# Statistics of two row tiles moved from VectorE to ScalarE, silu moved behind the first four statistics, and new orders for all engines

## The chip, the core and the metric

The kernel runs on one core of one Trainium2 chip. The metric is the device time of one execution in microseconds (us); of the kernel before there are three runs: 1036.51, 1036.54 and 1036.72 us, median 1036.54 us. Times inside the kernel are those of one profiled execution, counted from the start of its span.

## What is computed

The reference is one AdaLN block in fp32 over x of shape (4, 1024, 1024): a modulation, attention with one head of 256, and a linear layer with a low-rank addition. What matters here is the front:

```python
mod = (_silu(L0_c) @ L0_wmod).reshape(L0_c.shape[0], 6, 1, -1)
sa, ca, ga, sb, cb, gb = (mod[:, 0], mod[:, 1], mod[:, 2], mod[:, 3], mod[:, 4], mod[:, 5])
h = _layernorm(x, axis=-1) * (1 + ca) + sa          # mean and variance of each row
x = x + ga * _L0_attn_ref(h, Wqkv, bqkv, Wo, bo)    # q, k, v = h @ Wqkv + bqkv; softmax; Wo
h = _layernorm(x, axis=-1) * (1 + cb) + sb
x = x + gb * _L0_ffn_ref(h, ...)
```

## The kernel before

Each batch b (0 to 3) has eight row tiles t of 128 rows by 1024, in two chunks j of four tiles. Each fp32 product is made of three fp32r products, of high and low parts: ScalarE writes the high part (rounded), VectorE the low part (what is left), and TensorE multiplies high by high, low by high and high by low (lines 1420 to 1422). Every engine follows a list of steps written out by hand (PE_ORDER, DVE_ORDER, ACT_ORDER, SP_ORDER, POOL_ORDER; TensorE's entries also name one of four PSUM pairs, A to D, and the step that must have been emptied out of it). An engine takes its steps strictly in this order, and each waits on semaphores, so a step that waits holds back all that stand behind it.

The steps that matter for the front of the kernel, batch 0:

- SP_ORDER loads 512 KB at a time: LN (b, t) a row tile of x (line 799, places xs, probs and xr), Lwm (s, k) a piece of the modulation weights (line 783 for the scale, named s = 0 in the order, line 785 for the others), LT a piece of x with columns on the partitions (line 819), LWq a piece of Wqkv (line 790), LW of Wo (line 858). The first 57 SP steps end with LN (1, 4).
- VectorE: SI makes silu of c (lines 1141 to 1143), which TensorE needs for M0 (0); ST (b, t) makes mean and variance of a row tile (two bn_stats of 512 columns, line 1221, a bn_aggr, line 1224; semaphore stat_made); Z (b, j, k) subtracts the mean and multiplies by 1/std (lines 1239, 1243); MM0 (c) brings a quarter of the scale into place (line 1147, semaphore ca_made); WQL the low part of the weights (lines 1207, 1210); HL the low part of h (line 1249); BQ the biases of q, k, v.
- ScalarE: WQH the high part of weights (line 1014), MC0 copies the scale out of PSUM (line 993), HH the high part of h (line 1026), BMC and BPC copy the spread means and 1/std of chunk 1 (line 1001), KR copies k out of PSUM (line 1053), EX the exponentials of the softmax (line 1090).
- GpSimd: RS (b, j) makes 1/std of a chunk (lines 929, 931).
- TensorE: BCM (j) and BCP (j) spread mean and 1/std of chunk j over the partitions (line 1487; BCM (j) waits for the four statistics of the chunk, and chunk 0 includes tiles 0 to 3, chunk 1 tiles 4 to 7); M0 (c) and MT0 (c) make and turn a quarter of the scale (lines 1443, 1454); K0 (c) and V0 (c) are quarters of k and v of chunk 0 (lines 1567 and 1420 to 1422); M (s, r) and MT (s) make and turn the other modulation rows (lines 1465, 1473; r = 0 needs pieces 0 and 1, r = 1 pieces 2 and 3); Q, K, V (b, j, ...) are q, k, v; SAM and SAT the share of the shift in the biases; S, PT, PV and O the attention; PP and W the low-rank weights; T and F the second norm's turn and the last product.

The first V0 waits until the second quarter of the scale has left its PSUM pair (ca_made at least 2). The front runs, on TensorE: BCM0, M0 0, BCP0, MT0 0, M0 1, K0 0, MT0 1, M0 2, V0 0, MT0 2, K0 1, V0 1, M0 3, V0 2, MT0 3, K0 2, BCP1, BCM1, V0 3, M 1 0, M 1 1, Q 0 0 0 and so on.

## Time and profile before

| what | value |
|---|---|
| runs | 1036.51, 1036.54, 1036.72 us; median 1036.54 |
| the profiled execution | 1036.71 us, of which its span is 1034.9 |
| TensorE (PE) matmul busy | 1007.2 us, 97% of the span |
| VectorE (DVE) busy | 660.2 us, 64% |
| ScalarE (ACT) busy | 312.3 us, 30% |
| GpSimd (POOL) busy | 235.7 us, 23% |
| granted TensorE clock | 0.997 of full speed |

The page gives busy time for each engine; PE is the matmuls, PEld the weight loads beside them, SPq the DMA issues of the sync engine. In a timeline row the first number is the start, the second the duration in us, then engine, line, operation, output and inputs, and in brackets how long the engine was idle before it and what ended that.

### The profile page before, as it was taken

To read this page: it belongs to the slowest core of one execution; us is meant where nothing else is said; L and a number is where in the kernel's file an instruction comes from. 1 tells how busy PE (TensorE), PEld (TensorE's weight loads), DVE (VectorE), ACT (ScalarE), POOL (GpSimd) and SP (SyncE) were. 2 spreads that over 40 slices of the span, in tenths; PEclk is the share of its full clock that TensorE was granted. 3 is DMA by queue.
4 is the path that set the end of the run, shared out by engine and by line. 5 is a ranking of instruction groups with operands and counts; after the bars stand their busy time and mean duration, and the time that the engine had idled before them with its cause. 6 is when DMAs were issued, how large, how long until landed. Compare 5 with 4: busy or idle time off the path is not lost.

```text
span 1034.9 us, 13028 instructions
## 1 busy us (share of the span) xinstructions
PE 1007.2 (97%) x5213; PEld 830.1 (80%) x5213; DVE 660.2 (64%) x830; ACT 312.3 (30%) x468; POOL 235.7 (23%) x181
## 2 busy tenths in 40 slices
...
GB/s 364 391 325 304 250 241 135 281 235 188 59 1 161 125 198 128 1 112 133 142 151 142 49 153 233 220 146 224 185 222 84 247 178 183 128 231 157 114 78 65
DMA packets 54428, 180.23 MB, mean 174 GB/s; under 512 B 5872, under 2 KB 6432, under 8 KB 54368
## 3 DMA queue, kind: packets, MB, share of 16 engines
...
q8 instruction: 42, 0.69, 0.3%
q14 instruction: 18, 0.15, 0.1%
...
## 4 chain that ended last, share of the span: by engine, by line
PE 94%; SPq 2%; DMA 2%; DVE 1%; issue 0%; ACT 0%; DVEq 0%; ACTq 0%
PE pairA L1420 8%; PE pairA L1421 8%; PE pairA L1422 8%; PE pairD L1420 7%; PE pairD L1421 7%; PE pairD L1422 7%; PE pairC L1420 7%; PE pairC L1421 7%; PE pairC L1422 7%; PE pairB L1420 6%; PE pairB L1422 6%; PE pairB L1421 6%; DMA w_raw<-in_wqkv 2%; SPq L819 1%; PE pairB L1617 1%; PE pairB L1552 1%
## 5 line engine op out<-in xcount | busy, mean ns | idle before, releaser
L956 POOL TENSOR_TENSOR res<-res,row_bc 128x1024 f32<-128x1024 f32 x32 | 84.2, 2640 | 85.4 <-DMA res<-x_dram 76.7
L943 POOL TENSOR_TENSOR xr<-xr,row_bc 128x1024 f32<-128x1024 f32 x32 | 81.2, 2544 | 92.8 <-DMA xr<-in_x 92.3
L1420 PE MATMUL pairD<-w_hi,h_hi 128*128 128x256 f32 (+1 forms) x256 | 87.0, 340 | 0.0
L1421 PE MATMUL pairD<-w_lo,h_hi 128*128 128x256 f32 (+1 forms) x256 | 86.6, 338 | 0.0
L1422 PE MATMUL pairD<-w_hi,h_lo 128*128 128x256 f32 (+1 forms) x256 | 86.3, 337 | 0.0
L948 POOL DMA_DIRECT2D x_dram<-xr x32 | 18.1, 567 | 258.6 <-DVE xr L1326 258.6
L1420 PE MATMUL pairC<-w_hi,h_hi 128*128 128x512 f32 (+1 forms) x192 | 72.3, 377 | 3.2 <-DVE h_lo L1249 2.7
L1421 PE MATMUL pairC<-w_lo,h_hi 128*128 128x512 f32 (+1 forms) x192 | 71.9, 375 | 0.0
L1422 PE MATMUL pairC<-w_hi,h_lo 128*128 128x512 f32 (+1 forms) x192 | 71.7, 373 | 0.0
L1117 ACT ACTIVATE w_hi<-w_sum 128x1024 fp32r<-128x1024 f32 x32 | 33.9, 1060 | 119.6 <-DVE w_sum L1370 119.3
L1421 PE MATMUL pairA<-w_lo,h_hi 128*128 128x256 f32 (+1 forms) x192 | 65.0, 338 | 0.0
L1420 PE MATMUL pairA<-w_hi,h_hi 128*128 128x256 f32 (+1 forms) x192 | 64.8, 338 | 0.0
L1422 PE MATMUL pairA<-w_hi,h_lo 128*128 128x256 f32 (+1 forms) x192 | 64.8, 337 | 0.0
L1026 ACT ACTIVATE h_hi<-z_cols,modT 128x512 fp32r<-128x512 f32 x64 | 42.7, 715 | 42.3 <-DVE z_cols L1243 37.5
L1411 DVE TENSOR_TENSOR res<-res,gated 128x1024 f32<-128x1024 f32 x31 | 53.0, 1711 | 0.8 <-POOL res L956 0.3
L1420 PEld LDWEIGHTS pairD<-w_hi,h_hi 128*128 128x128 f32 x256 | 48.3, 189 | 5.8
L1421 PEld LDWEIGHTS pairD<-w_lo,h_hi 128*128 128x128 f32 x256 | 48.4, 189 | 5.5
L1422 PEld LDWEIGHTS pairD<-w_hi,h_lo 128*128 128x128 f32 x256 | 48.3, 189 | 5.5
L965 POOL DMA_DIRECT2D out_y<-res x31 | 23.4, 756 | 124.5 <-DVE res L1411 124.5
L1420 PE MATMUL pairB<-w_hi,h_hi 128*128 128x512 f32 x128 | 50.3, 393 | 0.0
L1422 PE MATMUL pairB<-w_hi,h_lo 128*128 128x512 f32 x128 | 50.1, 392 | 0.0
L1421 PE MATMUL pairB<-w_lo,h_hi 128*128 128x512 f32 x128 | 50.1, 392 | 0.0
...
## 6 DMA issues: line engine op xcount, KB each, us to landing
...
```

Source lines behind the costliest of these rows:

```text
L819: sp.dma_start(z_cols[j][:, c2, :], x_cols[b, j, :, c2, :]).then_inc(ld_cols[j][k], 16)
L943: nc.gpsimd.tensor_tensor(xt, xt, row_bc[:, :], ALU.add).then_inc(residual_made, 1)
L948: pool.dma_start(x1_dram[row:row + P, :], xr[:, t % 2, :]).then_inc(st_x1[t % 2], 16)
L956: nc.gpsimd.tensor_tensor(rt, rt, row, ALU.add).then_inc(residual2_made, 1)
L965: pool.dma_start(dst.rearrange("(t p) n -> p t n", p=P), res[:, slot, :].rearrange("p (t n) -> p t n", t=2)).then_inc(st_y[slot], 16)
L1026: nc.scalar.activation(h_hi[j][:, ct, :], z_cols[j][:, ct, :], ACT.Copy, scale=modT[:, PLACE[CA], b, ct:ct + 1]).then_inc(h0_hi_made, 1)
L1117: nc.scalar.activation(w2_hi[h][:, 2 * cp:2 * cp + 2, :], w_sum[:, n % 2, :].rearrange("p (c n) -> p c n", c=2), ACT.Copy).then_inc(w2_hi_ ...
L1411: nc.vector.tensor_tensor(res[:, slot, :], res[:, slot, :], gated[:, :], ALU.add).then_inc(y_made, 1)
L1420: nc.tensor.matmul(out, left[0], right[0], start=first, stop=False, skip_group_check=True)
L1421: nc.tensor.matmul(out, left[0], right[1], start=False, stop=False, skip_group_check=True)
L1422: return nc.tensor.matmul(out, left[1], right[0], start=False, stop=last, skip_group_check=True)
L1552: last = nc.tensor.transpose(ps[:, (2 * cc + k) * P:(2 * cc + k + 1) * P], xs[:, k, ct * P:(ct + 1) * P], ident)
```

## The change

VectorE gives up the statistics of tiles 5 and 7 of batch 0. ScalarE makes them in five instructions each: a copy of the tile onto itself that also sums it, mean and negated mean from the sum, a square of the tile minus its mean that also sums, and the variance. It uses two new semaphores and three columns of `total` as scratch. Since stat_made then counts 30 statistics and not 32, its waiters take their number from stat_no, and those that need tiles 5 or 7 also wait for act_stat_made. SI stands behind the first four ST on VectorE. All five orders are new: 414 steps of TensorE, 268 of SP and 152 of GpSimd are the same steps in another order. SP's first 57 steps stay in place.

```diff
+        ACT_STATS = (5, 7)
+        def stat_no(b, t):
+            return QT * b + t - sum(QT * b + t > k for k in ACT_STATS)
...
                 elif what == "LN":
-                        sp.wait_ge(stat_made, 6 if (b, t) == (1, 0) else QT * b + t)
+                        if (b, t) == (1, 0):
+                            sp.wait_ge(act_stat_made, 1)
+                        else:
+                            sp.wait_ge(stat_made, stat_no(b, t))
...
                 if what == "RS":
-                    pool.wait_ge(stat_made, QT * b + 4 * j + 4)
+                    pool.wait_ge(stat_made, stat_no(b, 4 * j + 4))
+                    if b + j > 0:
+                        pool.wait_ge(act_stat_made, 2)
...
+                elif what == "ST":
+                    t = i[1]
+                    place, turn = stat_place(0, t)
+                    no = ACT_STATS.index(t)
+                    rows = rows_at[place]
+                    act.wait_ge(ld_rows[place], 16 * turn)
+                    wait(act, act_stat_made, no)
+                    nc.scalar.activation(rows, rows, ACT.Copy, accum_out=sums[:, 0:1]).then_inc(act_stat_step, 1)
+                    act.wait_ge(act_stat_step, 4 * no + 1)
+                    nc.scalar.activation(stat[:, 1, 0, t % 4:t % 4 + 1], sums[:, 0:1], ACT.Copy, scale=1.0 / H).then_inc(act_stat_step, 1)
+                    nc.scalar.activation(sums[:, 1:2], sums[:, 0:1], ACT.Copy, scale=-1.0 / H).then_inc(act_stat_step, 1)
+                    act.wait_ge(act_stat_step, 4 * no + 3)
+                    nc.scalar.activation(rows, rows, ACT.Square, bias=sums[:, 1:2], accum_out=sums[:, 2:3]).then_inc(act_stat_step, 1)
+                    act.wait_ge(act_stat_step, 4 * no + 4)
+                    nc.scalar.activation(stat[:, 1, 1, t % 4:t % 4 + 1], sums[:, 2:3], ACT.Copy, scale=1.0 / H).then_inc(act_stat_made, 1)
...
                     if what == "BCM":
-                        pe.wait_ge(stat_made, 4 * j + 4)
+                        pe.wait_ge(stat_made, stat_no(0, 4 * j + 4))
+                        if j == 1:
+                            pe.wait_ge(act_stat_made, 2)
```

The front of three orders, as it becomes. TensorE:

```python
    ("BCM", (0,), "A", None), ("M0", (0,), "B", None), ("BCP", (0,), "A", None), ("MT0", (0,), "B", None),
    ("M0", (1,), "C", None), ("K0", (0,), "D", None), ("M0", (2,), "B", ("M0", 0)), ("MT0", (1,), "C", None),
    ("MT0", (2,), "B", None), ("V0", (0,), "C", ("M0", 1)), ("M0", (3,), "B", ("M0", 2)), ("K0", (1,), "D", None),
    ("MT0", (3,), "B", None), ("V0", (1,), "C", None), ("K0", (2,), "D", None), ("V0", (2,), "C", None),
    ("BCM", (1,), "A", ("BCM", 0)), ("K0", (3,), "D", None), ("BCP", (1,), "A", None),
    ("M", (1, 0), "B", ("M0", 3)), ("M", (1, 1), "B", None), ("Q", (0, 0, 0), "D", ("K", 0, 0)),
    ("M", (1, 2), "B", None), ("V0", (3,), "C", None), ("M", (1, 3), "B", None), ("Q", (0, 0, 1), "D", None),
```

VectorE (before, MM0 (1) stood ahead of WQL (1, 1), HL (0, 0, 3) behind WQL (0, 0)):

```python
    ("ST", (0, 0), None), ("ST", (0, 1), None), ("ST", (0, 2), None), ("ST", (0, 3), None), ("SI", (), None),
    ("Z", (0, 0, 0), "A"), ("MM0", (0,), "B"), ("WQL", (1, 0), None), ("HL", (0, 0, 0), None),
    ("WQL", (2, 0), None), ("Z", (0, 0, 1), "A"), ("WQL", (1, 1), None), ("MM0", (1,), "C"), ("MM0", (2,), "B"),
    ("HL", (0, 0, 1), None), ("Z", (0, 0, 2), "A"), ("WQL", (2, 1), None), ("ST", (0, 4), None),
    ("HL", (0, 0, 2), None), ("ST", (0, 6), None), ("Z", (0, 0, 3), "A"), ("MM0", (3,), "B"),
    ("HL", (0, 0, 3), None), ("WQL", (0, 0), None), ("WQL", (0, 1), None), ("Z", (0, 1, 0), None),
    ("Z", (0, 1, 1), None), ("ST", (1, 0), None), ("Z", (0, 1, 2), None), ("Z", (0, 1, 3), None),
```

Later on VectorE: ... VL (0, 1, 0), ST (1, 3), BQ, QL (0, 0, 0), ... ScalarE (before, WQH (0, 0) stood ahead of HH (0, 0, 3)):

```python
    ("WQH", (1, 0), None), ("MC0", (0,), "B"), ("HH", (0, 0, 0), None), ("WQH", (2, 0), None), ("MC0", (1,), "C"),
    ("WQH", (1, 1), None), ("MC0", (2,), "B"), ("HH", (0, 0, 1), None), ("WQH", (2, 1), None), ("MC0", (3,), "B"),
    ("HH", (0, 0, 2), None), ("ST", (0, 5), None), ("ST", (0, 7), None), ("HH", (0, 0, 3), None),
    ("WQH", (0, 0), None), ("WQH", (0, 1), None), ("BMC", (1,), "A"), ("KR", (0, 0, 0), "D"),
```

The last dozen steps of TensorE and the last dozen of VectorE are those of before, with other PSUM pairs, but for WL2 (3, 7), which changes place with a neighbour.

## Rows read from the trace of the kernel before

**Rows 1.** The page, busy time by engine.
```profile
PE 1007.2 (97%) x5213; PEld 830.1 (80%) x5213; DVE 660.2 (64%) x830; ACT 312.3 (30%) x468; POOL 235.7 (23%) x181
```

**Rows 2.** Waits of PE, whole span: us in total, times, longest.
```profile
PE pairA L1487 <- DVE stat L1224: 11.8, 1, 11.8
PE pairC L1420 <- DVE h_lo L1249: 2.7, 2, 1.6
PE pairD L1567 <- ACT h_hi L1026: 1.9, 1, 1.9
PE pairA L1643 <- DVE q_lo L1318: 0.5, 1, 0.5
...
PE pairC L1652 <- DVE w_sum L1370: 0.4, 1, 0.4
PE pairC L1420 <- DVE w_sum L1370: 0.4, 1, 0.4
```

**Rows 3.** Timeline of PE, start to 52 us: start, duration, instruction, idle before.
```profile
11.85 2.04 PE L1487 MATMUL pairA<-consts,stat 128*128 128x128 f32 x8 [11.85 <-DVE stat L1224]
...
25.26 0.39 PE L1420 MATMUL pairC<-w_hi,h_hi 128*128 128x256 f32 x1 [0.50 <-DVE modT L1147]
...
28.23 0.50 PE L1454 MATMUL pairB<-consts,row_bc 128*128 128x4 f32 x4
28.60 1.17 PE L1567 MATMUL pairD<-h_hi,w_hi 128*128 128x512 f32 x4
...
31.47 0.28 PE L1420 MATMUL pairC<-w_hi,h_hi 128*128 128x256 f32 x1
...
49.43 1.92 PE L1465 MATMUL pairB<-wm,pads 128*32 128x512 f32 x16
51.28 0.50 PE L1420 MATMUL pairA<-h_hi,w_hi 128*128 128x512 f32 x1
```

**Rows 4.** Timeline of VectorE, to 80 us.
```profile
5.98 1.28 DVE L1221 BATCH_NORM_STATS2 bn<-xs 128x6 f32<-128x512 f32 x2
...
25.04 0.16 DVE L1147 TENSOR_SCALAR modT<-pairC 128x8 f32<-128x8 f32 x1
25.72 1.23 DVE L1210 TENSOR_TENSOR w_lo<-w_raw,w_hi 128x1024 fp32r<-128x1024 f32 x1 [0.52 <-ACT w_hi L1014]
...
33.63 1.28 DVE L1221 BATCH_NORM_STATS2 bn<-xs 128x6 f32<-128x512 f32 x2
...
79.93 0.69 DVE L1221 BATCH_NORM_STATS2 bn<-xs 128x6 f32<-128x512 f32 x1 [9.38 <-DMA xs<-in_x]
```

**Rows 5.** Timeline of ScalarE: high part of weight piece (1, 1).
```profile
24.63 1.06 ACT L1014 ACTIVATE w_hi<-w_raw 128x1024 fp32r<-128x1024 f32 x1 [2.65 <-DMA w_raw<-in_wqkv]
```

**Rows 6.** Single lines: issues, first and last start, then time from issue to landing.
```profile
L799 SPq DMA_DIRECT2D xs<-in_x x1: 389/389/389, 0.7 to 0.7; - x1
...
DMA to landing us min/median/max: 4.0/4.4/4.8
```

**Rows 7.** The same for the fifth and sixth scale pieces, window 8.2 to 8.7.
```profile
L783 SPq DMA_DIRECT2D wm<-in_w_scale x2: 434/454/475, 7.8 to 8.3; - x2
DMA to landing us min/median/max: 14.2/14.6/15.0
```

**Rows 8.** The same for the last two of Lwm (1, 0) to (1, 3).
```profile
L785 SPq DMA_DIRECT2D wm<-in_wmod x2: 1076/2482/3887, 30.1 to 34.0; - x2
DMA to landing us min/median/max: 15.0/16.3/17.6
```

**Rows 9.** Timeline of SP's issues: row tile LN (1, 3).
```profile
71.10 0.45 SPq L799 DMA_DIRECT2D xs<-in_x  x1
```

**Rows 10.** Groups by line and shape, ScalarE: busy us, mean ns.
```profile
L1090 ACT ACTIVATE probs<-pairA,neg_max 128x1024 f32<-128x1024 f32 x9 | 10.0, 1114 | 9.8 <-DVE neg_max L1305 9.8
...
L1090 ACT ACTIVATION_READ_ACCUMULATOR probs<-pairA,neg_max 128x1 f32 x9 | 1.8, 197 | 0.0
...
L1123 ACT ACT_TABLE_LOAD x1 | 1.3, 1283 | 1.2 <-PEq L1678 1.2
```

More of the change, by code:

```diff
@@ L394 @@
     ("LT", 1, 0, 3), ("Lwm", 2, 4), ("Lwm", 2, 5), ("LN", 1, 3), ("Lwm", 2, 6), ("Lwm", 2, 7), ("LN", 1, 4),
-    ("Lwm", 3, 0), ("Lwm", 3, 1), ("SW", 1, 0), ("Lwm", 3, 2), ("Lwm", 3, 3), ("LN", 1, 5), ("LBC", 1, 0),
-    ("Lwm", 3, 4), ("Lwm", 3, 5), ("Lwm", 3, 6), ("Lwm", 3, 7), ("LN", 1, 6), ("Lwm", 4, 0), ("Lwm", 4, 1),
-    ("LN", 1, 7), ("RS_", 0), ("Lwm", 4, 2), ("Lwm", 4, 3), ("LN", 2, 0), ("Lwm", 4, 4), ("RS_", 1), ("Lwm", 4, 5),
-    ("SW", 1, 1), ("Lwm", 4, 6), ("Lwm", 4, 7), ("LN", 2, 1), ("LBC", 1, 1), ("Lwm", 5, 0), ("Lwm", 5, 1),
-    ("Lwm", 5, 2), ("Lwm", 5, 3), ("LN", 2, 2), ("Lwm", 5, 4), ("Lwm", 5, 5), ("LN", 2, 3), ("Lwm", 5, 6),
[14 rows of a table removed]
-    ("LW2", 1, 0), ("LRES", 0, 1, 0, 0), ("LW2", 1, 1), ("LRES", 0, 1, 0, 1), ("LRES", 0, 0, 1, 0),
[10 rows of a table removed]
+    ("SW", 1, 0), ("LN", 1, 5), ("LBC", 1, 0), ("LN", 1, 6), ("Lwm", 3, 0), ("Lwm", 3, 1), ("Lwm", 3, 2),
+    ("Lwm", 3, 3), ("LN", 1, 7), ("Lwm", 3, 4), ("Lwm", 3, 5), ("Lwm", 3, 6), ("Lwm", 3, 7), ("LN", 2, 0),
+    ("SW", 1, 1), ("RS_", 0), ("Lwm", 4, 0), ("Lwm", 4, 1), ("Lwm", 4, 2), ("LBC", 1, 1), ("Lwm", 4, 3),
+    ("LN", 2, 1), ("Lwm", 4, 4), ("Lwm", 4, 5), ("LN", 2, 2), ("Lwm", 4, 6), ("Lwm", 4, 7), ("Lwm", 5, 0),
+    ("Lwm", 5, 1), ("LN", 2, 3), ("Lwm", 5, 2), ("Lwm", 5, 3), ("Lwm", 5, 4), ("Lwm", 5, 5), ("LN", 2, 4),
[19 rows of a table added]
+    ("LRES", 1, 1, 1, 0), ("LX", 9), ("LW2", 2, 4), ("LRES", 1, 1, 1, 1), ("LRES", 2, 0, 0, 0),
[5 rows of a table added]
     ("LRES", 3, 0, 1, 0), ("LRES", 3, 0, 1, 1), ("LRES", 3, 1, 1, 0), ("LRES", 3, 1, 1, 1),
@@ L499, in build_block @@
         r_total = sb("r_total", [P, QT])
+        sums = total[:, 0:3]
         xs = sb("xs", [P, 2, H])
@@ L625, in build_block @@
         stat_made = sem("stat_made")
+        act_stat_made = sem("act_stat_made")
+        act_stat_step = sem("act_stat_step")
         stat_spread = sem("stat_spread")
@@ L823, in step @@
                     if n == 0:
-                        sp.wait_ge(stat_made, QT * B)
+                        sp.wait_ge(stat_made, stat_no(B, 0))
                         sp.wait_ge(z_made, 2 * 4 * B)
```

9 lines of the change are left out of this document (5 added, 4 removed), and 676 rows, old and new, of tables (ACT_ORDER, DVE_ORDER, PE_ORDER, POOL_ORDER).

## The prediction

> **What bounds the kernel now.** Read the page first: TensorE is busy for 1007.2 of 1034.9 us [rows 1], so an edit can only bring back the other 27.7 us, or add to them. The waits of TensorE say where they are [rows 2]: 11.8 us before its first matmul, then 1.9 + 0.5 + 2.7 = 5.1 us, each of them before its Q (0, 0, 0) at 51.28 [rows 3] (the 0.5 stands in the bracket of the row at 25.26), then 0.5 + 0.4 + 0.4 = 1.3 us around 590 to 627, where batch 3 ends and the F steps begin. The rest, 9.5 us, is nearly all the tail behind the last matmul; the last steps don't change, so it stays. From 51.28 to the first of the three late waits TensorE never waits: there the change can only lose. So I look at the time at which TensorE begins Q (0, 0, 0): before it stands, before and after, the same work but for two exchanges named below, and all that follows moves with it.
>
> The second reading is who feeds TensorE until then, and that is the DMA queue. Pieces of 512 KB are issued early and land long after, one every 1.3 us: the fifth and sixth scale pieces, issued at 7.8 and 8.3, land at 22.0 and 23.3 [rows 7]. The last piece that M (1, 1) needs is issued at 34.0 and lands at 49.0 [rows 8], and M (1, 1) stands just ahead of Q (0, 0, 0) in both orders. The issues up to there are the same and none is delayed, so with its last quarter (two matmul groups of 1.85 us for both M steps, 49.43 to 51.28 [rows 3], so 0.5 us for the last piece) Q can't begin before 49.5. **The most that the front can give is 51.28 - 49.5 = 1.8 us.**
>
> **Part 1: SI behind the first four statistics.** The first tile lands at 0.7 + 4.0 = 4.7 [rows 6], but the first statistics start at 5.98 [rows 4], behind SI, which waits for the exponential. From there to BCM (0) are 11.85 - 5.98 = 5.9 us. Started at 4.75, BCM (0) starts at 10.6: 1.25 us sooner. SI (0.7 us) then ends at 11.2, and M0 (0), its only user, comes behind BCM (0) (2.04 us [rows 3]), at 12.6: hidden by 1.4 us.
>
> **Part 2: the order of TensorE up to the first V0.** K0 (0) can go earlier, since MM0 (0) no longer stands behind a WQL: the 1.9 us wait goes. But M0 (2) now comes before MT0 (1), and waits for its pieces until 23.3. Then V0 (0) waits until MM0 (1) has emptied the pair, and on VectorE MM0 (1) now stands behind WQL (1, 1), whose weights land at 24.6: ScalarE 24.63, VectorE 25.72, 1.14 us until the next can start [rows 4, 5], so MM0 (1) at 26.86 and, with its 0.16 us and the hand-over (25.04 to 25.26 before [rows 3, 4]), **V0 (0) at 27.1 and not at 25.26: a new wait, 1.8 us later**. Queued behind WQL (1, 1) and MM0 (1) on VectorE are MM0 (2) and HL (0, 0, 1), for which M0 (3) and K0 (1) wait; they have V0 (0)'s 3.0 us of cover. MT0 (2) (0.4) is done inside the wait. So the gain of part 1 is lost here and comes back only with the later waits.
>
> **Part 3: from V0 (0) to Q.** Before, 51.28 - 25.26 = 26.0 us, of them 2.7 us waits for h_lo [rows 2], so 23.3 us work. After: less MT0 (2), 28.23 to 28.60, 0.37; V0 (3) is behind Q and K0 (3) ahead of it: less 2.97 (25.26 to 28.23), plus 2.87 (28.60 to 31.47) [rows 3]. That makes 22.85 us. Do the 2.7 us go? The first wait was for HL (0, 0, 2), behind two statistics; now one stands before it, and TensorE comes 0.8 us later. The second was for HL (0, 0, 3), behind WQL (0, 0) and so behind the landing of its weights; that is undone. What is late next is ScalarE: HH (0, 0, 3), BCM (1) and RS (0, 1) now wait for its statistics. No row shows a square with a sum. The nearest is the exponential over 1024 columns, 1.11 us, and its accumulator read, 0.2 [rows 10]; two of those and three small ones of some 0.2 to 0.3 give 3.5 us for a tile. At the low end (no reads) it is 3.1, at the high end a table load of 1.28 [rows 10] lies before each square and one behind it: 6.1. Tile 5 is there at 33.6 [rows 4] and tile 7 sooner than ScalarE is free, so both end at 40.6 (39.8 to 45.8 at the ends). TensorE comes to BCM (1) at about 43.2, counted back from Q at 50 through two M, BCP, K0 (3) and BCM: **covered by 2.6 us** at the middle value, short by 2.6 at the high end. LN (1, 0), which waits for ScalarE's tile 5 (37), stands in a DMA queue that is full until 49 anyway. The 2.8 us that VectorE is spared cost and save nothing by themselves: they are cover. So Q begins at 27.1 + 22.85 = 49.95, 0.45 after the DMA's bound: **1.3 us sooner**.
>
> **Part 4: the rest of the orders.** BPC (1) now comes behind K0 (3) and two KR, so Z (0, 1, 0) starts some 1.5 us later than before; HL (0, 1, 3) is wanted by V (0, 1, 0) behind SAM, and I find about 1 us of cover there. The three late waits: PP (0, 1) stood right behind PV (3, 0, 1) and is moved off, so 0.5 us goes; W (0, 3) and then O (3, 4) still follow the first WS closely, with two W's and the low part of O crowding before it, so I leave the 0.8 us and add 0.3. Net 0.2, not counted. SP's steps behind the 57th move by up to eight places, mostly row tiles ahead of modulation weights; POOL's by four at most (RS (3, 1) later); their users are tens of us away.
>
> **Sum.** The profiled execution is 1036.71 us, 1.8 more than its span. Span 1034.9 - 1.3 = 1033.6, execution 1035.4; the median of the runs is 0.17 lower, so **1035.2 us**, a gain of 0.13%. About 0.2% (2.07 us) is what a measurement of this kernel can tell from no change; I forecast less than that.
>
> **Rivals.**
> - *The late waits go as well, or TensorE packs better* (the new orders everywhere are for that): 1.3 to 1.8 in the front and all 1.3 later is 2.6 to 3.1 us, 1033.4 to 1033.9. For: PP's wait is undone. Against: the DMA's bound, and WS is still close.
> - *The gain is eaten by small new waits* past 51 us, where none were and 400 TensorE steps are in a new order: a few of 0.4 (the size seen for W) give 1036 to 1037. For: so many edits at so little idle.
> - *The row tile ahead of the biases*, ending slower. On VectorE ST (1, 3) now stands before BQ, and through QH and QL everything of q and k in batch 0 hangs on it; K (0, 1, 0) can't enter its pair before. Before, tile LN (1, 3) was issued at 71.1 [rows 9] and ST (1, 3) waited 9.4 us, until 79.93 [rows 4], at no cost. Now I step ST (1, 3) to 78.7, and TensorE to K (0, 1, 0) at 85.8, with 1.4 us of cover. A landing later than 80.1 costs TensorE each us; it must be past 81.4 to make the kernel slower and past 83.5 for over 0.2%. With an issue 2 to 4 us later than before (behind ST (1, 2)) it lands at 82 to 84; if the like happens in the next batch, 1037.5 to 1039.5. For: the 8.8 us from issue to landing. Against: the transfers before it are freed sooner.
> - *The square isn't in the loaded table.* The trace has one table load, of 1.28 us, for exponentials and copies together [rows 10]. If each square brings a load before and one after, ScalarE ends at 45.8, BCM (1) costs 2.6 us, and the kernel ends at 1037.8 (slower by 1.3). The Trainium skill, "ScalarE: Activation LUTs", section on table sets, speaks against this part of the change: functions come in sets with one expensive function each and cheap ones as filler, and a switch costs about 2.66 us with the drain; it doesn't say that square is among the fillers. By that figure, an estimate, four switches make 10.6 us, ScalarE ends at 51.2 and the kernel at 1043. No run shown here has a switch. The chance of this rival, 0.07, rests on rows: copies and exponentials of the whole kernel share one load.
>
> **How the numbers follow.** Forecast (1034.5 to 1036.1) 0.50; late waits too 0.15; gain eaten 0.15; row tile 0.13, of it 0.10 beyond 0.2%; table 0.07, of it 0.04 beyond. Faster by over 0.2%: 0.15. Slower: 0.10 + 0.04 = 0.14. Same: 0.71. The range reaches into the first rival and to the middle of the third: 1033.6 to 1038.2, which leaves out about 0.05 below and 0.10 above.
>
> **What would show it.** In the changed kernel's timeline: BCM (0) at 10.6; V0 (0) at 27.1 with a wait for modT of some 0.6 behind MT0 (2); no wait from there to Q (0, 0, 0) at 49.5 to 50; ScalarE's two tiles in 7 us with no second ACT_TABLE_LOAD; waits of TensorE for W at about 0.8 to 1.1. I am wrong if wmod's fourth piece lands at another time than 49.0, if there is a wait of TensorE between 51 and 590 of over 0.5 us, or if TensorE's busy time changes by more than 0.5 us by the order alone.

## The result, and the profile after

The changed kernel is slower: 1038.55 us median against 1036.71 us of the kernel before measured beside it, ratio 1.0015 (95% interval 1.0008 to 1.0022). The forecast was 1035.2, range 1033.6 to 1038.2, so the time lies outside the range and on its slow side. By the bound of 0.2% named there the change counts as within it; the sign and the size that I forecast are wrong. The profiled execution took 1038.47 us with a span of 1036.7; the forecast for it was 1035.4. So 3.07 us have to be found. One of the eleven timed runs of e10_fill7 took 3992 us and is left out everywhere below, which makes its median 1035.44 and not 1035.81.

The page of the kernel after, busy time by engine [rows 1]:

```profile
PE 1009.9 (97%) x5213; PEld 832.7 (80%) x5213; DVE 650.9 (63%) x822; ACT 318.5 (31%) x482; POOL 230.4 (22%) x181
```

TensorE has the same 5213 instructions and is busy for 2.7 us more. Nothing was added to it, so something took longer; what it was, this number doesn't say (e11_no_wait2 has 2.6 us more without the cause found here). The waits of TensorE over the whole span (total, times, longest), which answer to [rows 2]:

```profile
PE pairA L1520 <- DVE stat L1255: 10.8, 1, 10.8
PE pairB L1485 <- ACT row_bc L1007: 1.6, 1, 1.6
PE pairC L1474 <- DMA wm<-in_w_scale: 1.3, 2, 0.6
PE pairB L1474 <- DMA wm<-in_w_scale: 1.2, 2, 0.6
PE pairB L1650 <- ACT probs L1121: 1.1, 1, 1.1
PE pairB L1451 <- DVE w_sum L1401: 0.4, 1, 0.4
PE pairD L1451 <- DVE w_sum L1401: 0.4, 1, 0.4
PE pairA L1685 <- DVE w_sum L1401: 0.4, 1, 0.4
PE pairC L1451 <- DVE xr L1357: 0.3, 1, 0.3
```

The waits for h_lo are gone, as is the one for q_lo. New are the waits for the scale pieces (2.5 us), the one of 1.55 us before MT0 (2), and, late in the kernel, one of 1.1 us for the probabilities. The timeline of TensorE, from its first matmul to Q (0, 0, 0), which answers to [rows 3]:

```profile
10.79 0.98 PE L1520 MATMUL pairA<-consts,stat 128*128 128x128 f32 x3 [10.79 <-DVE stat L1255]
...
26.30 0.98 PE L1485 MATMUL pairB<-consts,row_bc 128*128 128x4 f32 x4 [1.55 <-ACT row_bc L1007]
27.27 0.58 PE L1451 MATMUL pairC<-w_hi,h_hi 128*128 128x256 f32 x1
27.65 0.42 PE L1452 MATMUL pairC<-w_lo,h_hi 128*128 128x256 f32 x1
27.87 0.41 PE L1453 MATMUL pairC<-w_hi,h_lo 128*128 128x256 f32 x1
...
32.31 1.06 PE L1474 MATMUL pairB<-wm,pads 128*32 128x256 f32 x15
...
51.74 0.50 PE L1451 MATMUL pairD<-h_hi,w_hi 128*128 128x512 f32 x1
```

The start is as forecast: BCM (0) at 10.79 (10.6), V0 (0) at 27.27 (27.1). Then it goes wrong inside V0 (0): its matmuls of 256 columns follow each other at 0.21 us instead of 0.12, MT0 (2) ahead of it takes 0.98 us where it took 0.50 [rows 3], and V0 (0) lasts from 27.27 to 32.31, 5.04 us, where it lasted 25.26 to 28.23, 2.97 us. The same stretch by windows; the last columns are the granted clock, the DMA share and GB/s. Of the kernel before:

```profile
24.00:26.00 2.00, 1.50 (x22) 0.93 (x15) 1.48 (x3) 1.37 (x2) 0.00 (x0) 1.00 1.03 420
26.00:28.00 2.00, 2.00 (x19) 2.00 (x18) 2.00 (x3) 1.18 (x3) 0.00 (x0) 1.00 1.02 408
```

and of the kernel after:

```profile
22.00:24.00 2.00, 1.07 (x16) 0.34 (x16) 1.97 (x3) 0.00 (x0) 0.00 (x0) 1.00 1.01 414
24.00:26.00 2.00, 0.74 (x8) 0.52 (x4) 0.51 (x2) 1.18 (x2) 0.00 (x0) 0.74 1.04 418
26.00:28.00 2.00, 1.70 (x7) 1.66 (x8) 1.38 (x3) 0.84 (x3) 0.00 (x0) 0.50 1.03 410
28.00:30.00 2.00, 2.00 (x12) 2.00 (x10) 1.93 (x3) 0.70 (x3) 0.00 (x0) 0.50 1.03 410
30.00:32.00 2.00, 2.00 (x12) 2.00 (x12) 1.97 (x3) 1.00 (x1) 0.00 (x0) 0.56 1.03 406
```

TensorE's granted clock goes from 2.4 to 1.2 GHz (0.50) in the window 24 to 26 and comes back in the window 30 to 32. With 0.74 and 0.56 as means of the two levels, that is 1.04 us at half in the first and 1.76 us in the last: low from 25.0 to 31.8. Just before it, TensorE worked 1.07 of 2 us and then sat in the new wait, which begins at 24.75: MT0 (2) needs ScalarE's copy MC0 (2) (25.79), and that stands behind WQH (1, 1), whose weights ScalarE could take only at 24.82. In the profile of the kernel before the clock stays at 1.00 there. The Trainium skill, "TensorE: Matmul & The Clock Gate", section "What's actually happening", says that a gate halves the array's clock by how busy the engine has been of late; by that rule a wait has a second price behind it, and this trace agrees. It doesn't come behind every wait, as e3 shows below.

The other loss is late. ScalarE around 567 us, start, duration, instruction, idle before:

```profile
564.38 1.03 ACT L1126 ACTIVATE h_hi<-pairB 128x1024 fp32r<-128x1024 f32 x1 [1.49 <-PE pairB L1650]
567.64 1.06 ACT L1135 ACTIVATE a_stack<-a_raw 128x1024 fp32r<-128x1024 f32 x1 [2.23 <-DMA b_raw<-in_lora_b]
568.60 1.04 ACT L1136 ACTIVATE b_stack<-b_raw 128x1024 fp32r<-128x1024 f32 x1
569.55 1.09 ACT L1121 ACTIVATE probs<-pairC,neg_max 128x1024 f32<-128x1024 f32 x1
```

The step TLA (both copies of the LoRA rows) now stands ahead of EX (3, 2). It waits for a transfer and then copies, 4.2 us in all, the exponentials stand behind it, and TensorE comes to the transposes of the probabilities 1.08 us too early. In the order of before the same wait of TLA is longer (3.7 us) but stands behind EX (3, 3), and TensorE has other work.

**The account of the profiled execution.** Q (0, 0, 0) at 51.74 instead of the 49.95 forecast: 1.79. Waits of TensorE behind 52 us: 1.08 + 0.30 + 0.39 + 0.40 + 0.44 = 2.61 instead of 1.33: 1.28. Together 3.07, the whole of the difference.

### The profile page after: what moved, and what is told of

Same layout as the page of the kernel before. It is cut to its first block, busy times and chain, and to the rows that moved or that the text cites. A ratio compares the mean times of both kernels' runs of the same rounds, so it can differ in the third digit from the quotient of the medians.

```text
span 1036.7 us, 13036 instructions
## 1 busy us (share of the span) xinstructions
PE 1009.9 (97%) x5213; PEld 832.7 (80%) x5213; DVE 650.9 (63%) x822; ACT 318.5 (31%) x482; POOL 230.4 (22%) x181
## 4 chain that ended last, share of the span: by engine, by line
PE 91%; DMA 4%; DVE 2%; issue 1%; SPq 1%; ACT 0%; POOL 0%; DVEq 0%; ACTq 0%; POOLq 0%
PE pairC L1451 8%; PE pairC L1452 8%; PE pairC L1453 8%; PE pairA L1452 7%; PE pairA L1451 7%; PE pairA L1453 7%; PE pairB L1451 6%; PE pairB L1452 6%; PE pairB L1453 6%; PE pairD L1451 6%; PE pairD L1452 6%; PE pairD L1453 6%; DMA w_raw<-in_wqkv 2%; DMA xs<-in_x 1%; PE pairD L1585 1%
## 5 line engine op out<-in xcount | busy, mean ns | idle before, releaser
L1451 PE MATMUL pairA<-w_hi,h_hi 128*128 128x512 f32 (+1 forms) x256 | 90.4, 353 | 0.0
L1452 PE MATMUL pairA<-w_lo,h_hi 128*128 128x512 f32 (+1 forms) x256 | 89.9, 351 | 0.0
L1453 PE MATMUL pairA<-w_hi,h_lo 128*128 128x512 f32 (+1 forms) x256 | 89.8, 351 | 0.0
L1451 PE MATMUL pairB<-w_hi,h_hi 128*128 128x512 f32 (+1 forms) x208 | 71.6, 344 | 0.4 <-DVE w_sum L1401 0.4
L1452 PE MATMUL pairB<-w_lo,h_hi 128*128 128x512 f32 (+1 forms) x208 | 71.3, 343 | 0.0
L1453 PE MATMUL pairB<-w_hi,h_lo 128*128 128x512 f32 (+1 forms) x208 | 71.1, 342 | 0.0
L1451 PEld LDWEIGHTS pairA<-w_hi,h_hi 128*128 128x128 f32 x256 | 48.3, 189 | 6.7
L1453 PEld LDWEIGHTS pairA<-w_hi,h_lo 128*128 128x128 f32 x256 | 48.3, 189 | 6.7
L1452 PEld LDWEIGHTS pairA<-w_lo,h_hi 128*128 128x128 f32 x256 | 48.4, 189 | 6.5
L1280 DVE SCALAR_TENSOR_TENSOR h_lo<-z_cols,modT,h_hi 128x512 fp32r<-128x512 f32 x64 | 44.3, 745 | 2.5 <-ACT h_hi L1056 2.5
```

What stands on the lines that cost most here:

```text
L1280: nc.vector.scalar_tensor_tensor(h_lo[j][:, ct, :], z_cols[j][:, ct, :], modT[:, PLACE[CA], b, ct:ct + 1], h_hi[j][:, ct, :].bitcast(F32), ...
L1451: nc.tensor.matmul(out, left[0], right[0], start=first, stop=False, skip_group_check=True)
L1452: nc.tensor.matmul(out, left[0], right[1], start=False, stop=False, skip_group_check=True)
L1453: return nc.tensor.matmul(out, left[1], right[0], start=False, stop=last, skip_group_check=True)
```

## The experiments

All times are medians with the kernel before measured beside them on the same chip (1036.7 to 1037.0 in each group). "Late" is the sum of TensorE's waits behind 52 us in the profiled execution, "half clock" the stretch at 1.2 GHz there, behind the start and ahead of the kernel's tail. "Clock of the timed runs" is the mean of the granted clock over all timed runs; the kernel before has 0.9963 to 0.9966 beside them. As there are only two levels, 0.001 of it stands for some 2.1 us at half (an estimate: 0.001 x 1036 x 2). The single runs of one kernel lie 1 to 5 us apart and the intervals of the ratios are +-0.001, so differences under about 0.7 us are read from profiles only, and each of those is one execution.

| run | median us | ratio to before (95%) | Q (0,0,0) at | late us | half clock, us | clock of the timed runs |
|---|---|---|---|---|---|---|
| kernel after | 1038.55 | 1.0015 (1.0008 to 1.0022) | 51.74 | 2.61 | 25.0 to 31.8 | 0.9949 |
| e8_again (kernel after) | 1038.74 | 1.0023 (1.0013 to 1.0032) | 50.88 | 3.38 | 26.6 to 30.0 | 0.9942 |
| e1_filler | 1038.07 | 1.0010 (1.0001 to 1.0019) | 49.93 | 3.68 | 571 to 574 | 0.9964 |
| e2_mm0 | 1037.48 | 1.0006 (0.9998 to 1.0015) | 49.75 | 4.86 | 571 to 575 | 0.9961 |
| e3_si | 1037.16 | 1.0003 (0.9994 to 1.0012) | 50.91 | 0.95 | none | 0.9955 |
| e4_small | 1035.35 | 0.9983 (0.9975 to 0.9992) | 49.74 | 1.77 | 18.5 to 21.9 | 0.9968 |
| e14_small_again | 1035.42 | 0.9986 (0.9977 to 0.9995) | 50.20 | 1.65 | none | 0.9975 |
| e7_dve_stats | 1037.14 | 1.0001 (0.9992 to 1.0010) | 51.67 | 1.64 | 38.5 to 41.9 | 0.9946 |
| e5_tla | 1035.89 | 0.9991 (0.9982 to 1.0000) | 51.01 | 1.59 | 26.8 to 30.3 | 0.9943 |
| e12_tla_again | 1036.39 | 0.9997 (0.9989 to 1.0006) | 49.76 | 2.34 | 18.7 to 22.1 | 0.9948 |
| e6_tla_filler | 1035.48 | 0.9987 (0.9979 to 0.9996) | 49.85 | 1.75 | none | 0.9963 |
| e10_fill7 | 1035.44 | 0.9987 (0.9978 to 0.9997) | 50.11 | 1.23 | none | 0.9973 |
| e13_fill7_again | 1035.11 | 0.9984 (0.9975 to 0.9993) | 49.72 | 2.72 | none | 0.9972 |
| e9_no_wait | 1040.76 | 1.0037 (1.0023 to 1.0050) | 50.16 | 5.53 | 88.5 to 95.3 | 0.9932 |
| e11_no_wait2 | 1034.93 | 0.9983 (0.9974 to 0.9992) | 49.97 | 1.44 | none | 0.9967 |

**1. Is it the clock? Fill the idle time (e1_filler).** The theory: the clock fell because TensorE was too idle. The rival: the order of the transfers or ScalarE's statistics made Q late.

```diff
     ("K0", (0,), "D", None),
+    ("WU", (4,), "B", ("M0", 0)),
     ("M0", (2,), "B", ("M0", 0)), ("MT0", (1,), "C", None),
+    ("WU", (7,), "C", None),
     ("MT0", (2,), "B", None),
+    ("WU", (2,), "C", None),
     ("V0", (0,), "C", ("M0", 1)),
...
-                    for _ in range(5):
+                    for _ in range(i[0]):
```

> The changed kernel with idle TensorE time filled: 13 matmuls of 512 columns whose result nobody reads (4 ahead of M0 (2), 7 behind MT0 (1), 2 behind MT0 (2)); no other step moves. Theory C (the granted clock fell to half from 24.9 to 31.8 us because TensorE had worked too little before it, and V0 (0) was done at half speed): the clock stays at 1.00, V0 (0) starts at 27.2 to 27.5 as in the changed kernel but takes 3.0 us and not 5.1, Q (0, 0, 0) begins at 49.9 to 50.2 instead of 51.74, the late waits stay at 2.6 us, and the profiled execution comes to 1036.7 to 1037.0 (1.6 us under the changed kernel, equal to the kernel before). Theory O (the late Q comes from the order: row tiles ahead of modulation weights, or ScalarE's statistics, and the clock is only a companion): Q stays at 51.7 and the time at 1038.4.

The front came out as theory C says: V0 (0) starts at 26.99, its matmuls follow each other at 0.12 us, and Q begins at 49.93, 1.81 us sooner than in the kernel after, though TensorE had 13 matmuls more to do. The rival is out. But the time hardly moved (0.5 us): the front's gain was given back at 570 us. The wait for the probabilities grew to 1.81 us, and right behind it the clock fell there too (windows, and the wait on TensorE's timeline):

```profile
568.00:570.00 2.00, 0.48 (x5) 0.51 (x6) 1.97 (x3) 2.00 (x4) 0.00 (x0) 1.00 0.00 0
570.00:572.00 2.00, 1.96 (x14) 1.75 (x13) 1.08 (x3) 1.50 (x3) 0.00 (x0) 0.71 0.13 47
572.00:574.00 2.00, 2.00 (x7) 1.62 (x6) 1.52 (x3) 1.02 (x1) 0.00 (x0) 0.50 1.10 360
...
569.52 1.07 PE L1644 MATMUL pairB<-consts,probs 128*128 128x128 f32 x8 [1.81 <-ACT probs L1115]
```

From Q to TensorE's last matmul this run took 977.79 us, without its waits 974.11; the kernel after took 975.65, without its waits 973.04. The fall at 571 so cost 1.07 us against this profile; against e8_again (972.65), a second profile of the kernel after, it is 1.46, so its size is known to some 0.4 us. I had expected the late waits to stay at 2.6: that part of the forecast was wrong.

**2. Take the wait away instead (e2_mm0).** Which idle time brings the clock down, the wait of 1.55 us or the thin work ahead of it?

```diff
 DVE: -    ("WQL", (1, 1), None), ("MM0", (1,), "C"), ("MM0", (2,), "B"), ("HL", (0, 0, 1), None),
      +    ("MM0", (1,), "C"), ("WQL", (1, 1), None), ("HL", (0, 0, 1), None), ("MM0", (2,), "B"),
 PE:  -    ("MT0", (2,), "B", None), ("V0", (0,), "C", ("M0", 1)),
      +    ("V0", (0,), "C", ("M0", 1)), ("MT0", (2,), "B", None),
```

> The changed kernel with the new wait ahead of V0 (0) taken away: MM0 (1) again ahead of WQL (1, 1) on VectorE, MM0 (2) behind HL (0, 0, 1), and V0 (0) ahead of MT0 (2) on TensorE. V0 (0) can start at 25.0 to 25.3. Theory C1 (the clock falls because of the 1.55 us wait): it stays at 1.00, Q (0, 0, 0) begins at its bound by the transfers, 49.5, the span is 2.2 us shorter than the changed kernel's, 1034.5, time 1036.3. Theory C2 (the clock falls at 24.9 because of the thin work before the wait, with M0 (2) held by its pieces): nothing before 24.74 differs, so it falls at 24.9 all the same, the slow stretch costs V0 (0) and M0 (3) 3.2 us, and Q begins at 51.5 to 51.8, time 1038.2 to 1038.5. Theory O (order of the transfers): Q at 51.7 with the clock at 1.00.

C1 held in the front: V0 (0) at 24.36, clock 1.00, Q at 49.75 and so at the transfers' bound: the last piece for M (1, 1) lands at 48.73, and from there Q takes 1.02 us. The time was 1037.5 in the median and 1039.9 in the profiled execution, not 1036.3: the same wait at 570 (1.89, with a fall of the clock behind it), and one that the prediction had as a rival, the row tile ahead of the biases:

```profile
86.86 0.50 PE L1444 MATMUL pairD<-h_hi,w_hi 128*128 128x512 f32 x1 [1.74 <-DVE q_lo L1304]
```

That is K (0, 1, 0). Behind this wait of 1.74 us the clock stayed at 1.00. In the kernel after ST (1, 3) started at 81.22, as its tile landed, and K (0, 1, 0) at 86.87, 0.25 us behind the end of QL (0, 0, 1): nothing was lost only because TensorE was late itself.

**3. The parts of the change, alone (e3_si, e4_small, e7_dve_stats).** All three start from the kernel before.

```diff
 e3, e7 and e4, DVE:
-    ("SI", (), None), ("ST", (0, 0), None), ("ST", (0, 1), None), ("ST", (0, 2), None), ("ST", (0, 3), None),
+    ("ST", (0, 0), None), ("ST", (0, 1), None), ("ST", (0, 2), None), ("ST", (0, 3), None), ("SI", (), None),
 e7 and e4, DVE and ACT:
-    ("WQL", (1, 0), None), ("MM0", (0,), "B"),
+    ("MM0", (0,), "B"), ("WQL", (1, 0), None),
-    ("WQL", (0, 0), None), ("HL", (0, 0, 3), None),
+    ("HL", (0, 0, 3), None), ("WQL", (0, 0), None),
-    ("WQH", (0, 0), None), ("HH", (0, 0, 3), None),
+    ("HH", (0, 0, 3), None), ("WQH", (0, 0), None),
 e4 alone, with the new code of the change; DVE, then ACT:
-    ("ST", (0, 4), None), ("ST", (0, 5), None), ("HL", (0, 0, 2), None), ("ST", (0, 6), None), ("ST", (0, 7), None),
+    ("ST", (0, 4), None), ("HL", (0, 0, 2), None), ("ST", (0, 6), None),
-    ("MC0", (3,), "B"),
+    ("MC0", (3,), "B"), ("ST", (0, 5), None), ("ST", (0, 7), None),
```

> The kernel before with SI alone moved behind the first four statistics. BCM (0) starts at 10.7 to 10.8 instead of 11.85 and M0 (0) 1.1 us sooner. M0 (1) and K0 (0) then wait for their scale pieces and for the low half of the K weights, which don't come sooner, so the 1.1 us are given back as waits before K0 (0) at 20.3. Main theory: Q (0, 0, 0) at 51.3 +-0.1, time equal to before within 0.2 us, clock 1.00. Rival (the early statistics are worth their 1.1 us by themselves): Q at 50.2, time 1035.6. Rival C (a longer idle stretch before K0 (0), 3.0 us of 1.9, brings the clock down): some granted clock of 0.5 between 18 and 30 and Q at 52 or later.

Q at 50.91, 0.37 sooner than before, time equal to that of before (1037.16 against 1036.97). Of the 1.47 us gained at BCM (0) (10.38), 0.86 is left at V0 (0) (24.40 against 25.26); then the wait for HL (0, 0, 2) is longer:

```profile
37.36 0.36 PE L1414 MATMUL pairC<-w_hi,h_hi 128*128 128x256 f32 x1 [2.71 <-DVE h_lo L1243]
```

It was 1.09 us before, and V0 (3) starts at 46.01 against 46.38. So the time is given back, but at another place than I had written. The main theory held but for that and the 0.4 us at Q; the first rival wanted Q at 50.2, and the second fell in this profile (the timed runs' clock, 0.9955 against 0.9966, leaves room for a fall in some of them). The row shows more: TensorE waited 2.71 us and the granted clock stayed at 1.00 behind it (windows 36 to 42), so a long wait doesn't bring the clock down each time.

> The kernel before with only those parts of the change that the front needs: SI behind the first four statistics, MM0 (0) ahead of WQL (1, 0), statistics of tiles 5 and 7 on ScalarE, and HH and HL (0, 0, 3) ahead of the first q weights' halves; every other order as before. Main theory (all of the gain sits in the front and is limited by the transfer that lands at 49.0): K0 (0) has no 1.9 us wait, both waits for h_lo go, Q (0, 0, 0) at 49.5 to 49.7, the three late waits 1.3 us as before, clock 1.00, time 1.6 to 1.8 us under the kernel before, 1034.9 to 1035.1. Rival (theory C again: idle in the front shows up as a fall of the clock): Q at 50.5 to 52. Rival (gain is given back later): Q at 49.6, but waits behind 51 us that sum to 1 us or more.

Q at 49.74 and 1.6 us faster than before. The clock did fall, from 18.5 to 21.9, behind the thin M0 (1):

```profile
18.00:20.00 2.00, 1.75 (x10) 0.98 (x11) 2.00 (x4) 1.04 (x2) 0.00 (x0) 0.62 1.02 408
20.00:22.00 2.00, 2.00 (x6) 1.52 (x6) 1.97 (x3) 0.85 (x2) 0.00 (x0) 0.52 1.04 418
```

K0 (0) took 4.2 us (19.08 to 23.26) where e14 took 2.9 at full clock, and at Q it cost nothing: against e14, which had no fall, M0 (2)'s two waits for its pieces (0.45 and 0.55) are gone, V0 (0) starts at 24.70 instead of 24.04, and the wait for HL (0, 0, 2), which ends at 36.10 here and at 36.13 there, takes the rest. This fall came where TensorE had slack, and cost nothing.

> The small version a second time (median 1035.35, lowest spread of all: 1034.6 to 1036.0). Its medians should agree within 0.3 us; the stretch at half clock in its first profile (18.5 to 21.9) lies where TensorE has slack, so Q (0, 0, 0) is at 49.7 to 49.9 with or without it.

It repeated: 1035.42, no fall, Q at 50.20 (0.3 later than I had written: the last piece for M (1, 1) landed at 49.17 and not at 48.72).

> The small version of the change without its new code: all statistics on VectorE, but SI behind the first four, MM0 (0) ahead of WQL (1, 0), HH and HL (0, 0, 3) ahead of the halves of the q weights. If ScalarE's statistics are what takes the wait for HL (0, 0, 2) from 2.7 to 1.15 us, that wait is 2.4 to 2.7 us here, Q (0, 0, 0) begins at 50.4 to 50.9 instead of 49.74, and the time lies 0.7 to 1.1 us over the small version, 1036.0 to 1036.5. If the orders alone do it, Q at 49.7 and 1035.3.

Without ScalarE's statistics the wait for HL (0, 0, 2) is 2.57 us instead of 1.15 and 1.35, and the kernel is no faster than before: 1037.14, and with each set against the kernel before beside it 1.5 to 1.8 over the two measurements of the small version. Of that, the profile shows 1.2 to 1.4 as the wait and the rest behind it: the clock fell from 38.5 to 41.9, in the middle of V0, and Q began at 51.67 instead of the 50.4 to 50.9 expected. The timed runs fit: their granted clock is 0.9946 against 0.9968 and 0.9975. The orders of e7 and e4 differ only in who makes the statistics of the two tiles, so ScalarE's passes are what pays in this change, 1.5 to 1.8 us, where I had called them cover.

**4. The kernel after once more (e8_again).** Is the fall an accident of one execution?

> The changed kernel itself once more, for a second profile and as the neighbour of the next runs on the same chip. Theory C (clock): the work ahead of 24.9 us is set by the transfers and by the order, so the granted clock should fall to 0.50 again in the front, between 24 and 32 us, and Q (0, 0, 0) should begin at 51.5 to 52; the wait before PT (3, 1) should be 0.8 to 1.5 us again. Rival (the fall was an accident of one execution): clock 1.00 in the front and Q at 49.9 to 50.2, and then the lost 1.8 us are not a property of the kernel. Median 1038.0 to 1038.8.

It fell again, later and for half as long:

```profile
24.00:26.00 2.00, 0.64 (x8) 0.52 (x4) 0.19 (x1) 1.28 (x2) 0.00 (x0) 1.00 1.03 412
26.00:28.00 2.00, 1.48 (x8) 1.42 (x9) 1.22 (x4) 0.84 (x3) 0.00 (x0) 0.64 1.02 408
28.00:30.00 2.00, 2.00 (x11) 2.00 (x11) 2.00 (x3) 0.70 (x2) 0.00 (x0) 0.50 1.03 412
```

Q at 50.88, so against e1's 49.93 the fall cost 1.0 us here and 1.8 in the first profile. The wait at 570 was 1.45.

**5. The late step (e5_tla) and both repairs (e6_tla_filler).**

```diff
 ACT: -    ("PH", (3, 1), "B"), ("TLA", (), None), ("EX", (3, 2), "C"), ("EX", (3, 3), "A"), ("PH", (3, 2), "B"),
      +    ("PH", (3, 1), "B"), ("EX", (3, 2), "C"), ("EX", (3, 3), "A"), ("PH", (3, 2), "B"), ("TLA", (), None),
 DVE: -    ("TLL", (), None), ("PL", (3, 2), "B"), ("PL", (3, 3), "C"),
      +    ("PL", (3, 2), "B"), ("PL", (3, 3), "C"), ("TLL", (), None),
```

> The changed kernel with one late step moved: on ScalarE the two copies of the LoRA rows (TLA) stand three steps later, behind EX (3, 2), EX (3, 3) and PH (3, 2), and their partner TLL on VectorE behind PL (3, 3). Theory L (the wait of 1.08 us before PT (3, 1) is the wait of TLA for b_raw plus its copies, ahead of EX (3, 2)): that wait goes, TensorE's waits behind 52 us sum to 1.3 to 1.6 us instead of 2.6, and the time is 1.0 us under the changed kernel's. The first 52 us don't change. Rival (TensorE is met by the next late step at once): a new wait of 0.5 us or more between 565 and 580, time within 0.3 us of the changed kernel's.

The wait at 570 is gone and nothing took its place. ScalarE at the same point (compare the fence of the kernel after):

```profile
563.49 1.03 ACT L1119 ACTIVATE h_hi<-pairB 128x1024 fp32r<-128x1024 f32 x1 [1.50 <-PE pairB L1643]
564.41 1.11 ACT L1114 ACTIVATE probs<-pairC,neg_max 128x1024 f32<-128x1024 f32 x1
...
570.74 1.05 ACT L1128 ACTIVATE a_stack<-a_raw 128x1024 fp32r<-128x1024 f32 x1
```

The median fell by 2.85 us against e8_again beside it, not by 1.0; the second measurement (e12), set against the kernel before, makes it 2.1. The wait is 1.1 to 1.9 us. A fall of the clock behind it, as in the profiles of e1 and e2, could make up the rest, but the timed runs don't show it: their granted clock is the same with the wait at 570 (0.9949 and 0.9942) as without it (0.9948 and 0.9943), and so it is for e1 against e6 (0.9964 and 0.9963). The rest, up to 1 us, stays open.

> Both repairs at once: the 13 filler matmuls in the front and TLA three steps later. If the clock in the front (1.8 us) and TLA (1.1 to 1.8 us) are the two causes, nothing is left of the loss: Q (0, 0, 0) at 49.9, no granted clock of 0.5 near 570 (the fall there in the first filler run came right behind the 1.8 us wait), waits behind 52 us 1.2 to 2.0 us, profiled execution 1034.9 to 1035.9, that is 2.5 to 3.5 us under the changed kernel and 1 to 1.5 under the kernel before: the 1035.2 of the forecast. If the gain of the front is always given back behind it (transfers that land at their own time), the time stays at 1037 or more and new waits of the lost length stand between 52 and 1025 us.

Q at 49.85, no fall ahead of the tail, span 1032.9, median 1035.48: 3.3 us under the kernel after, 1.4 under the kernel before. With the two causes taken away, the forecast gain is there (1.3 us forecast, 1.4 measured).

**6. Which idle, and what it costs in timed runs (e10_fill7, e12_tla_again, e13_fill7_again).** Both kernels have TLA later; e10 and e13 have in addition only the seven matmuls in the 1.55 us wait.

> The changed kernel with TLA later (as measured before, Q (0, 0, 0) at 51.01, clock at half from 26.9 to 30.3) and only 7 filler matmuls, in the 1.56 us wait behind MT0 (1); the small waits of 0.4 to 0.65 us for the scale pieces between 15 and 24 us stay. Theory C1 (the 1.56 us wait is what brings the clock down): clock 1.00 in the front, Q at 49.8 to 50.0, time 0.4 to 1.2 us under that version's 1035.9. Theory C2 (the small waits before it do): a stretch at 0.50 between 24 and 32 us all the same, Q at 50.8 or later.

C1 held: no fall in the front, and Q at 50.11. Of the four small waits for scale pieces only two were there, though (0.41 and 0.54); all four (0.69, 0.65, 0.40 and 0.54) stand in e13, again without a fall, and only that rules out C2. But the median (1035.44) lay only 0.4 us lower than that of e5 (1035.89), measured on another chip: not settled, so both were run again side by side.

> The changed kernel with TLA later, a second time (clock at half from 26.9 to 30.3 in its first profile, Q at 51.01, median 1035.89). If the fall is a property of the order, the second profile has it too, for 3.4 or 6.8 us between 24 and 32, with Q at 50.8 to 51.8; median 1035.6 to 1036.2.

> The same with the 7 filler matmuls, a second time (no fall in its first profile, Q at 50.11, median 1035.81). If the clock in the front costs timed runs what it costs profiled ones, this median is 0.9 to 1.8 us below that of its neighbour without filler; if it costs timed runs little (the fall comes in part of the executions only, or hides behind transfers), the two medians differ by less than 0.5 us.

Now 1036.39 against 1035.11: the filler gave 1.28 us. The first pair gave 0.4, so the front's clock costs timed runs some 0.8 us in the mean of the two pairs. That the timed runs have such falls too is on record: the granted clock of the timed runs is 0.9943 and 0.9948 with the wait left empty, 0.9973 and 0.9972 with the seven matmuls in it, 5 to 6 us less at half. e12's profile says why it scatters: there the clock fell from 18.7 to 22.1, where it costs nothing, and Q began at 49.76. I had expected the fall between 24 and 32. Over all profiles: of the four of an order with the 1.55 us wait left empty, three have a fall between 25 and 32 and one at 18.7; of the seven in which that wait is filled or gone, none has a fall in the first 85 us. The waits of 0.8 to 0.9 and 0.65 us for the scale pieces at 17 and 18, behind which it fell in e4 and e12, stand in e1, e5, e9 and others too, without a fall. e13 showed K (0, 1, 0) waiting again, 1.11 us, with its tile landing at 80.75:

```profile
86.21 0.50 PE L1445 MATMUL pairD<-h_hi,w_hi 128*128 128x512 f32 x1 [1.11 <-DVE q_lo L1305]
```

**7. All repairs without extra work (e9_no_wait, e11_no_wait2).** e5 and e2 together, and ST (1, 3) moved.

```diff
 DVE:
-    ("ST", (1, 3), None), ("BQ", (), "C"), ("QL", (0, 0, 0), "D"), ("KL", (0, 0, 0), None), ("KL", (0, 0, 1), None),
-    ("QL", (0, 0, 1), "D"), ("VL", (0, 1, 1), "B"),
 in e9:
+    ("BQ", (), "C"), ("QL", (0, 0, 0), "D"), ("KL", (0, 0, 0), None), ("KL", (0, 0, 1), None),
+    ("QL", (0, 0, 1), "D"), ("VL", (0, 1, 1), "B"), ("ST", (1, 3), None),
 in e11:
+    ("BQ", (), "C"), ("QL", (0, 0, 0), "D"), ("KL", (0, 0, 0), None), ("KL", (0, 0, 1), None),
+    ("QL", (0, 0, 1), "D"), ("ST", (1, 3), None), ("VL", (0, 1, 1), "B"),
```

> All repairs without any extra work: TLA and TLL later as in the run before, MM0 (1) and V0 (0) earlier so that the 1.56 us wait ahead of V0 (0) is not there, and ST (1, 3) behind QL (0, 0, 1) and VL (0, 1, 1) on VectorE. Theory: no granted clock of 0.50 before 1020 us, Q (0, 0, 0) at 49.7 to 49.8, no wait before K (0, 1, 0) (1.74 us in the version with MM0 (1) alone), none before PT (3, 1), late waits 1.2 to 1.7 us, profiled execution 1034.9 to 1035.6, median 1.3 to 2.0 us under the kernel before. Rival for K (0, 1, 0) (the wait there is not ST (1, 3)'s tile but the copies of q and k themselves): the wait of 1 to 2 us stays.

The wait before K (0, 1, 0) went, but I had not asked who else waits for ST (1, 3): RT0 (1, 0) does, through POOL's scale, and behind VL (0, 1, 1) it came 4.3 us late. Towards the end of that wait the clock fell (88.5):

```profile
89.73 0.37 PE L1520 MATMUL pairC<-consts,stat 128*8 128x128 f32 x1 [4.31 <-POOL stat L938]
...
88.00:90.00 2.00, 0.27 (x2) 0.26 (x3) 0.20 (x2) 0.00 (x0) 1.21 (x2) 0.62 0.36 72
90.00:92.00 2.00, 2.00 (x6) 1.61 (x6) 0.39 (x1) 0.26 (x1) 0.00 (x0) 0.50 0.48 193
92.00:94.00 2.00, 2.00 (x6) 1.52 (x6) 1.10 (x4) 0.00 (x0) 0.00 (x0) 0.50 0.00 0
```

From Q to the end, waits taken off, this run took 974.7 us and e11 972.5: the fall cost 2.2 us on top of the 4.3.

> The version without the front's wait, mended: ST (1, 3) stands right behind QL (0, 0, 1) and ahead of VL (0, 1, 1), since behind VL it held RT0 (1, 0) for 4.3 us. Theory: q_lo is there at 82.5 as in the version before, the statistics of the tile end at 84.1, POOL's scale for them about 1.5 us later, so RT0 (1, 0) waits 0 to 0.4 us and K (0, 1, 0) not at all; Q (0, 0, 0) at 49.8 to 50.2, no fall of the clock before 1020 us, waits behind 52 us 1.2 to 1.7, profiled execution 1034.5 to 1035.5. Rival (V (0, 1, 1) or K (0, 1, 0) waits for what the statistics now delay): a wait of 1 to 1.7 us between 80 and 95, time 1036 to 1037.

Waits of TensorE in this version, whole span:

```profile
PE pairA L1513 <- DVE stat L1248: 10.4, 1, 10.4
PE pairB L1467 <- DMA wm<-in_w_scale: 0.5, 1, 0.5
PE pairB L1489 <- DMA wm<-in_wmod: 0.5, 2, 0.2
PE pairB L1444 <- DVE w_sum L1394: 0.4, 1, 0.4
```

The 0.5 us for in_wmod is the transfers' bound itself, at M (1, 0) and M (1, 1). Median 1034.93, the lowest of all, 1.76 us under the kernel before and 3.6 under the kernel after; the runs don't tell it from e13 and e4. It held the expectation. One row of it bears on the busy time at the start of this account: e11 has no fall ahead of its tail, and yet TensorE is busy for 1009.8 us, 2.6 more than before.

```profile
14.27 2.08 PE L1513 MATMUL pairA<-consts,stat 128*128 128x128 f32 x8
```

That is BCP (0), 1.16 us in the kernel before. The first matmuls of every profile run at half pace (M0 (0) takes 1.9 us in the kernel before, M0 (2) 1.07), and here this lasted through BCP (0); the windows don't show it, since the record of the clock begins only where it first rises. The two M (1, ...) took 3.7 us of busy time instead of 1.92, since they run as their pieces land. And e5, which has a fall, is busy for only 1008.1.

## Why the prediction was wrong, point by point

- **Part 1 (SI) right.** BCM (0) at 10.79 and between 10.27 and 10.56 in the other versions (10.6); the tile's statistics start at 4.92 (4.75).
- **Part 2 right in its times, not in who waits.** MM0 (1) at 27.05 (26.86), V0 (0) at 27.27 (27.1). But MT0 (2) isn't done inside the wait: the 1.55 us stand ahead of it, for ScalarE's MC0 (2) behind WQH (1, 1), and V0 (0) then has no wait for modT of 0.6. That both chains hang on the same weights is why the start came out. The price of the wait was taken as its length and no more.
- **Part 3, the term "22.85 us from V0 (0) to Q": this step failed.** Without the fall it is 22.94 us in e1 and 22.91 in e13. It took for granted that TensorE runs it at full clock, since the kernel before does. The kernel after spent 4.5 us of it at half, V0 (0) took 2.07 us more, and Q began 1.79 late. M0 (1), M0 (2) and V0 (0) all wait in the new order, and I summed the waits and did not look at the granted clock at all. No row of before shows a fall ahead of the tail, so none could have given its size; it could have stood as a rival.
- **The bound by the transfers was 0.5 us too early, and that hid in the sum.** The fourth wmod piece landed at 49.0 as forecast (48.6 to 49.2 in all profiles). But from its landing Q takes 1.02 us (48.72 to 49.74 in e4, 48.91 to 49.93 in e1, 49.17 to 50.20 in e14), not 0.5, so with 49.0 Q can't begin before 50.0, and the front could give 1.3 us, not 1.8. In e1 the two M take 2.34 us instead of 1.92 because they wait for pieces, so the work from V0 (0) to Q is some 22.5 us, 0.35 less than my term. That the forecast of 49.95 is met by e1, e6 and e13 within 0.25 us is therefore the bound's doing: luck, as far as the term is concerned.
- **ScalarE's statistics: mechanism right, price high.** A tile takes 2.97 and 2.99 us (3.5 forecast, low end 3.1), and both end at 41.0 (40.6). The square with its sum is 1.15 + 0.18 us:

```profile
34.96 1.05 ACT L1032 ACTIVATE xs<-xs 128x1024 f32<-128x1024 f32 x1
35.91 0.19 ACT L1032 ACTIVATION_READ_ACCUMULATOR xs<-xs 128x1 f32 x1
36.13 0.20 ACT L1034 ACTIVATE stat<-total 128x1 f32<-128x1 f32 x1
36.24 0.19 ACT L1035 ACTIVATE total<-total 128x1 f32<-128x1 f32 x1
36.46 1.15 ACT L1037 ACTIVATE xs<-xs,total 128x1024 f32<-128x1024 f32 x1
...
L1154 ACT ACT_TABLE_LOAD x1 | 1.3, 1283 | 1.2 <-PEq L1711 1.2
```

- **The table rival fell**: still one load in the whole kernel (last line above), and none of the squares waits for one.
- **"The 2.8 us that VectorE is spared are cover" was half wrong.** They are what shortens the wait for HL (0, 0, 2): 1.5 to 1.8 us in e4 and e14 against e7.
- **Part 4 failed too, in one place.** Of the three waits known before, the forecast was right: PP's 0.54 went, the rest grew to three of 0.4. I looked for moved steps only around those three, though TLA stood in the ScalarE order, moved ahead of two exponentials with a transfer to wait for. It was put at nothing, cost 1.08 us in the profiled execution, and is the term with the larger effect in timed runs: 2.1 to 2.85 us.
- **The rival "row tile" was right as a mechanism** and took no effect in the kernel after, because TensorE was late. As soon as the front is repaired it costs 1.74 (e2) and 1.11 (e13), when the tile lands at 81.4 and 80.75, and nothing when it lands by 79.4 (e1, e6, e10). Both costs point to the same limit, 79.65 (80.75 - 1.11 and 81.4 - 1.74), against 80.1 in the prediction.
- **The rival "gain eaten by small new waits" is the nearest to what came**, but its price was taken from W's 0.4. One wait of 1.1 to 1.9 us, and the clock in the front, are more than that.
- Of the signs named for being wrong, two came true: a wait over 0.5 between 51 and 590, and busy time off by more than 0.5 (2.7) with the instructions the same. The third didn't: wmod's fourth piece landed at 49.0.
